# Loops written out, and GpSimd's add of a chunk's residual moved one chunk later in the feed-forward stages

## The reference, cut to what matters

```python
h = norm(x) * (1 + scale) + shift            # shift, scale, gate from the condition
x = x + gate * attention(h)
h = norm(x) * (1 + scale) + shift
x = x + gate * feed_forward(h)               # block 0: gelu(h W1 + b1) W2 + b2
                                             # block 1: (silu(h w1) * (h w3)) w2
                                             # block 2: gelu, and then a gated linear unit
```

## Time and profile before

| | |
|---|---|
| median of 3 runs | 2075.79 us (2071.45 to 2076.36) |
| the profiled execution's own time | 2075.19 us |
| its span | 2073.4 us |
| TensorE busy | 1872.6 us (90% of the span) |
| VectorE, ScalarE, GpSimd busy | 1380.5, 1028.9, 799.0 us |
| mean granted TensorE clock | 0.968 of full speed |
| instructions in the profile | 42326 |

### The profile page before, as it was taken

The page is one execution under the profiler, slowest core; times in us unless marked ns, Lnnn a source line. Parts: engine busy times, 40 slices in busy tenths (PEclk is TensorE's granted clock), DMA queues, the critical chain, the costliest instruction groups (busy, mean ns, idle before and its releaser), DMA issues. The chain is left out here.

```text
span 2073.4 us, 42326 instructions
## 1 busy us (share of the span) xinstructions
PE 1872.6 (90%) x16038; PEld 1464.3 (71%) x16038; DVE 1380.5 (67%) x2128; ACT 1028.9 (50%) x1793; POOL 799.0 (39%) x737
## 2 busy tenths in 40 slices
PE   5999999999979998688988899978999889998998
PEld 4778777877867776466766677756777677776775
DVE  4665666566655665588898577767889756664555
ACT  3544444444447665366666344324555556663332
POOL 1210211021123445557668233446777824450000
PEclk8999999999989999799999999989999999999999
DMA  5100000000010000100000000010000000003322
GB/s 187 72 2 2 2 2 2 2 2 2 2 50 13 0 0 1 46 2 3 2 2 2 28 0 0 0 41 2 2 0 2 2 31 0 0 1 91 107 77 82
DMA packets 26596, 44.58 MB, mean 22 GB/s; under 512 B 4289, under 2 KB 12289, under 8 KB 26305
## 3 DMA queue, kind: packets, MB, share of 16 engines
q1 hardware_dynamic: 25152, 42.01, 6.1%
q10 hardware_dynamic: 1280, 0.23, 0.1%
HBM read 35.94 MB, written 6.29 MB: 20 GB/s over the span
## 5 line engine op out<-in xcount | busy, mean ns | idle before, releaser
L1230 DVE TENSOR_TENSOR Glb<-Gfb,Ghb 128x512 fp32r<-128x512 f32 x176 | 155.7, 894 | 67.0 <-ACT Ghb L1181 65.3
L449 PE MATMUL bank<-HH,W1b 128*128 128x512 f32 x448 | 184.8, 413 | 16.0 <-PEq L1538 7.1
L325 POOL TENSOR_TENSOR Tm<-Dv,MOD 128x512 f32<-128x512 f32 x94 | 108.4, 1173 | 204.6 <-DVE Dv L388 128.9
L451 PE MATMUL bank<-HH,W1b 128*128 128x512 f32 x448 | 177.2, 396 | 0.0
L450 PE MATMUL bank<-HL,W1b 128*128 128x512 f32 x448 | 177.0, 395 | 0.0
L449 PE MATMUL O<-Ghb,W2b 128*128 128x512 f32 x352 | 141.0, 400 | 31.7 <-DVE Glb L1230 31.6
L469 POOL TENSOR_TENSOR spare<-RT 128x1 f32<-128x1 f32 x32 | 11.4, 355 | 397.9 <-DVE RT L460 397.9
L314 POOL TENSOR_TENSOR XS<-Tm 128x512 f32<-128x512 f32 x48 | 70.1, 1460 | 214.5 <-ACT Tm L280 209.6
L451 PE MATMUL O<-Ghb,W2b 128*128 128x512 f32 x352 | 138.0, 392 | 0.0
L450 PE MATMUL O<-Glb,W2b 128*128 128x512 f32 x352 | 137.6, 391 | 0.0
L669 DVE COPY VP<-bank 64x256 f32<-64x256 f32 x128 | 54.0, 422 | 114.0 <-PE bank L632 112.7
(11 more groups left out here) (266 smaller groups left out, 5278.2 us busy)
## 6 DMA issues: line engine op xcount, KB each, us to landing
w<-l_w_dram SPq DMA_DIRECT2D x33, 256.0 KB, 3.4
X<-xT_dram SPq DMA_DIRECT2D x16, 256.0 KB, 6.7
out_dram<-XO SPq DMA_DIRECT2D x8, 512.0 KB, 2.7
wm<-w_mods_dram SPq DMA_DIRECT2D x4, 768.0 KB, 5.0
W2b_f<-l_w_dram SPq DMA_DIRECT2D x11, 256.0 KB, 5.2
WQK_f<-l_wqk_dram SPq DMA_DIRECT2D x8, 256.0 KB, 7.3
W1b_0f<-l_w_dram SPq DMA_DIRECT2D x8, 256.0 KB, 3.6
wm<-w_mods_dram SPq DMA_DIRECT2D x4, 384.0 KB, 6.7
```

The source lines that it names most:

```text
L325: nc.gpsimd.tensor_tensor(Tm[:, k].rearrange("p (b t) -> p b t", t=T), Dv[:, k].rearrange("p (b t) -> p b t", t=T), m, ALU.mult).then_inc( ...
L449: nc.tensor.matmul(out, w_lo_ap, x_hi, start=first, stop=False)
L451: return nc.tensor.matmul(out, w_hi_ap, x_hi, start=False, stop=last)
L1230: nc.vector.tensor_tensor(Gl[m % gb][:], gf, Gh[m % gb][:].bitcast(F32), ALU.subtract).then_inc(g_lo.h, 1)
```

## The change

It has two parts. All loops over chunks are written out in full, so that there is no jump and no loop variable, and each chunk's number is a constant. And in the feed-forward stages GpSimd adds the residual of chunk c-1 during chunk c, after its sum of squares, in place of adding chunk c's own at the end of its list for chunk c (that is, as soon as RT is there, ahead of the `pool_h` of the next turn). The last chunk does both: the add of chunk 6 after its sum of squares, then `nxt.fills` (constants for the next stage), then its own add. Attention 0 calls `residual_pool` as before.

```diff
-        def chunks(eng, body, unrolled=False):
-
-            if unrolled:
-                for c in range(NCH):
-                    body(c, c % 2, 2 if c < NCH - 2 else NCH - 1 - c)
-                return
-            with eng.Fori(0, NCH // 2 - 1) as j:
-                body(2 * j, 0, 2)
-                body(2 * j + 1, 1, 2)
-            body(NCH - 2, 0, 1)
-            body(NCH - 1, 1, 0)
+        def chunks(body):
+
+            for c in range(NCH):
+                body(c, c % 2, 2 if c < NCH - 2 else NCH - 1 - c)
...
                             if f:
                                 f.pool_ss(pool, cc)
                                 f.pool_sql(pool, cc)
+                            if c:
+                                residual_pool(pool, c - 1)
                             if more == 1 and wt:
                                 wt.low(pool, wt.all())
                             if not more:
                                 nxt.fills(pool)
-                            residual_pool(pool, c)
+                                residual_pool(pool, c)
                         if not gate:
-                            chunks(pool, body)
+                            chunks(body)
...
-                    body(0, 0, 2)
-                    with eng.Fori(0, NCH // 2 - 2) as j:
-                        body(2 * j + 1, 1, 2)
-                        body(2 * j + 2, 0, 2)
-                    body(NCH - 3, 1, 2)
-                    body(NCH - 2, 0, 1)
-                    body(NCH - 1, 1, 0)
+                    for c in range(NCH):
+                        body(c, c % 2, 2 if c < NCH - 2 else NCH - 1 - c)
```

More of the change, by code:

```diff
@@ L825, in _ @@
                         mod_transposes(pe, 2)
-                        chunks(pe, steps(step, lambda c: None))
+                        chunks(steps(step, lambda c: None))
                     @block.scalar
@@ L895, in _ @@
                         st.weights.high(act, 4)
-                        chunks(act, steps(step, lambda c: None))
+                        chunks(steps(step, lambda c: None))
                     @block.vector
@@ L1004, in _ @@
                         dve.wait_ge(x_in[2].h, x_in[2].at(16 * DH * (NCH - 2)))
-                        chunks(dve, steps(step, residual))
+                        chunks(steps(step, residual))
                         step_v.pending = step_c.n[0]
@@ L1165, in body @@
                                     f.pe_mean(pe, cc)
-                        chunks(pe, body, gate)
+                        chunks(body)
                     @block.scalar
@@ L1209, in body @@
                                     wt.high(act, 1)
-                        chunks(act, body, gate)
+                        chunks(body)
                     @block.vector
@@ L1269, in body @@
                                 residual_dve(dve, c, l, G_M, bcol_out, O2)
-                        chunks(dve, body, gate)
+                        chunks(body)
                     @block.gpsimd
@@ L1517, in ahead, with steps @@
                     return more >= 1 if tail else t + n < TL or more >= 1
-                def steps(eng, step):
+                def steps(step):
                     def body(c, p, more):
@@ L1653, in _ @@
                         step(0, 0, 0, 2, first=True)
-                        steps(pe, step)
+                        steps(step)
                         out_t(pe, NT - 1)
@@ L1721, in _ @@
                         step(0, 0, 0, 2, first=True)
-                        steps(act, step)
+                        steps(step)
                         oh(NT - 1, 1)
@@ L1799, in _ @@
                         fr.dve_norm(dve, 1)
-                        steps(dve, step)
+                        steps(step)
                         for tt in (NT - 2, NT - 1):
@@ L1835, in _ @@
                         step(0, 0, 0, 2, first=True)
-                        steps(pool, step)
+                        steps(step)
                         add(NCH - 1, 1)
```

## The result

The changed kernel takes 2037.51 us (median of 4 runs, 2036.93 to 2042.36), the kernel before on the same chip 2073.62 (4 runs, 2071.30 to 2076.36). The profiled execution took 2037.17 us, its span is 2035.3.

What follows compares the result with a forecast made beforehand. TensorE, busy 90% of the span, bounds the kernel; only its idle time can be won. 9.1 (b2) + 8.8 (b0) + 1.3 (b1) + 5.0 (jumps) + 0.3 = 24.5 us off 2075.19 (median 2075.79): predicted 2051, range 2042 to 2061.

Steps and rivals of the forecast that it cites:

- The collision with line 380: GpSimd's residual add blocks VectorE's Newton multiply, stopping TensorE 1.51 us; moving it wins 8.8 us in b0, 9.1 b2, 1.3 b1.
- Its new place: Add behind the sum of squares: group 6's low half goes first, group 7's has 1.8 us to spare; b1 only 0.5.
- the lost race: Rival, 15%: the moved add starts before group 6's low half; 0.8 us wait in some 10 b0/b2 chunks, 2059 us.
- The end of b0: Chunk 7 ends on GpSimd, which also gets the add of chunk 6; the stage's end moves by +0.9 us.
- The jumps: Jumps back in loops cost 3.4 us in attention 0 and 1.6 in attention 1, nothing elsewhere; together 5.0 us.
- The failed step: Saved register operations lie beside the engines' work, 0 to 2 us, counted 0.3; fewer ScalarE table loads give 0.
- straight code that starves TensorE: Rival, 3%: fetching written-out code stops TensorE about 2.2 us in each formerly looped attention chunk; 2087 us, slower.
- a wait of RT for the add: Rival, 2%: VectorE waits for the add before RT in some chunks, 1 us in each of 20; 2071 us.
- The larger gain "2044": Rival, 8%: the clock falls less often and more of the register work counts; 2044 us.

## Why the prediction was wrong

- **The collision with line 380** was read rightly and its term, 19.2 us for all three stages, came out at 19.1. That it fits so well is luck: errors inside it cancel. By stages b0 gave 9.6 (8.8 forecast), b2 11.0 (9.1), b1 cost 0.7 (1.3 forecast as won, -2 named as the worst). A stop costs 1.79 us, not the 1.51 that the row shows. TensorE's timeline of the kernel before, around one:

```profile
656.98 0.39 PE L450 MATMUL bank<-HL,W1b 128*128 128x512 f32 x1
657.21 0.39 PE L451 MATMUL bank<-HH,W1b 128*128 128x512 f32 x1
659.10 0.50 PE L449 MATMUL O<-Ghb,W2b 128*128 128x512 f32 x1 [1.51 <-DVE Glb L1230]
659.44 0.40 PE L450 MATMUL O<-Glb,W2b 128*128 128x512 f32 x1
```

  Products start every 0.23 us, though each is shown as 0.39 long; the idle time counts from that later end. From start to start the stop is 1.89 - 0.23 = 1.66, and the first product behind it holds the next one for 0.34 in place of 0.23: about 1.78, the 1.79 by which the chunk got shorter.
- **Its new place** held in the steady chunks: 0.73 us for group 6, 2.52 for group 7, and no cost (24.04 us with and without the add). In b1 every other steady chunk gains (with the add alone 26.5 became 26.1 us, the ones between stay at 25.9), but in chunk 6 the lost race makes a stop of 3 us out of one of 1.3. The margins had been read from a steady chunk alone; chunks 6 and 7, whose other work delays the sums, were not looked at.
- **The end of b0** is on GpSimd, as forecast; chunk 7 got 1.6 us longer (38.3 to 39.9), 0.9 were forecast. Putting the fills elsewhere gives 3.5 us.
- **The jumps**: 5.0 forecast, 5.2 measured by TensorE's list alone, with its register operations in it. What TensorE does in such a stop, a fetch or something else, no run here shows.
- **The failed step is the one behind it**: "The register operations that go ... lie beside the engines' work ... I take 0 to 2 us and count 0.3. Fewer table loads on ScalarE ... lie where ScalarE idles: 0." The loops were worth 17.5 us and not 5.3; the missing 12.2 are the 11.6 us of the result and more. The largest share, 6.1 us, lies in b1. There ScalarE's table load waited for a product that it didn't need, so 1.28 us of load stood behind the product and ahead of the function. Writing out ScalarE's list alone gave 4.6 us in b1, and putting that wait back into the changed kernel cost 7.0 us there. The register operations did not all lie beside the work either: on VectorE they delayed RT by 0.2 us in each gelu chunk, at a row that the prediction had before it. The reading "ScalarE idles here, so a saved load is free" was wrong, since what ScalarE makes next starts a chain (the multiply, both halves, VectorE's Newton steps behind them, GpSimd's `pool_h`) on which TensorE waited 8 times. The prediction counted only three waits of TensorE in b1, 1.7 us; the same view had these eight, 7.2 us.
- **Its evidence was no evidence.** "Written-out chunks of the kernel before run no faster than looped ones" compares chunks 6 and 7, which have other work and longer periods anyway (28.33 and 29.91 us in b1, from stop to stop), with the steady ones.
- **Of the rivals**, straight code that starves TensorE did not come (the adds of the changed kernel's attention 0 are 67.8 us apart, 68.0 was the one span without a jump), nor did a wait of RT for the add. The race was lost in b1's chunks 6 and 7; in the gelu stages TensorE's stops are the same, to 0.01 us, with the add and without it. The larger gain "2044", at 8%, pointed at the register work but was too small.
- **Left open**: most of the 14.7 us of VectorE's and GpSimd's loops. In the gelu chunks it is the wait ahead of RT, in the steady chunks of b1 a part of TensorE's wait for the low half, though not which register operation makes it. The 2.4 in attention 2 and the 4 us that the medians have beyond the profiled execution were not isolated. Beyond the jumps, what attention 0 and 2 gave is within the 3 us by which equal code varies.

## What to carry to other kernels

In this program a wait whose value depends on a loop's variable stood by itself in front of whatever came next, a table load too: look at each table load in a loop for idle time with a releaser, and see that the wait ahead of it is over early (7 us in b1, by the order of two lines). Such a collision as that of the add and line 380 is found by one line's shortest and median duration; here it was cured by another place in the list, and not by cutting the instruction. A new place has to be looked at in the first and last chunks too, not in a steady one alone. Idle engines are free only if nothing that waits for their next result is late; before costing an edit there at nothing, follow that result to the engine that bounds.

## What the chip showed beside it

The idle time in TensorE's row understated the stop: 1.51 us shown, 1.79 lost. A SCALAR_TENSOR_TENSOR with two inputs in SBUF is held like the multiply (1.67 us, line 382 with the add in halves). The Trainium skill (SBUF — State Buffer, section Who interferes with whom) says that the order of issue decides who blocks; the trace agrees to 0.03 us (1309.26 against 1309.29, 2.85 us). The Trainium skill (ScalarE: Activation LUTs, section What ACT_TABLE_LOAD costs) gives 1283 ns for the load, as measured here, and about 1380 ns more for a drain at each switch; the trace does not agree with the second here: the load starts at 1214.84, 0.01 us behind the exponential's end, and the function 0.07 us behind the load.
